# Two self attentions with scores issued first, and half of the output projection inside the second one

## The reference

```python
x = x + _L0_xattn_ref(_layernorm(x), ctx_1024, ...)
x = x + _L0_attn_ref(_layernorm(x), ...)     # "first attention": tokens of equal position attend to each other
x = x + _L0_ffn_ref(_layernorm(x), ...)      # 8 experts
x = x + _L1_xattn_ref(_layernorm(x), ctx_1024, ...)
x = x + _L1_attn_ref(_layernorm(x), ...)     # "second attention": the 64 tokens of a sample attend to each other
x = x + _L1_ffn_ref(_layernorm(x), ...)      # gated, inputs and weights rounded to FP4 by blocks of 16

def _L0_attn_ref(x, ...):
    ...
    scores = where(tril, q k^T / 4, -inf)
    out = softmax_one(scores) v              # e / (1 + sum e), no projection
def _L1_attn_ref(x, ...):
    ...
    out = softmax(q k^T / 4) v
    return out @ w_proj + b_proj
```

## Time and profile before

| what | us |
|---|---|
| median of 3 runs | 1421.54 (1418.49 to 1425.13) |
| the profiled execution | 1413.35 |
| its span in the trace | 1411.5 |
| PE busy | 1248.7 (88%) |
| DVE busy | 962.5 (68%) |
| ACT busy | 759.8 (54%) |
| POOL busy | 644.3 (46%) |

### The profile page before, as it was taken

One profiled execution on the slowest core, in us unless ns is written; L12 is line 12 of the kernel. 1 busy time (PEld: TensorE's weight loads), 2 busy tenths in 40 slices (PEclk: granted clock), 3 DMA queues, 4 the chain that ended last, 5 costly groups with the idle time before them and its releaser, 6 DMA issues. The chain is left out here.

```text
span 1411.5 us, 34690 instructions
## 1 busy us (share of the span) xinstructions
PE 1248.7 (88%) x12166; PEld 1044.0 (74%) x12166; DVE 962.5 (68%) x1990; ACT 759.8 (54%) x1379; POOL 644.3 (46%) x581
## 2 busy tenths in 40 slices
PE   5799999999999689449997799999999998667778
PEld 3588888888887557348885588888888887546446
DVE  5577777777777475465515677777777777576896
ACT  2577777777777211111224577777777776124121
POOL 2566656656654214042431556656656654315200
PEclk9999999999999885559999899999999999887999
DMA  6677777777765170435536677776776764100000
GB/s 199 173 205 196 176 194 188 181 195 182 185 170 126 42 55 2 127 119 177 187 131 190 176 201 182 186 201 176 182 205 176 183 173 111 35 1 3 0 4 26
DMA packets 106724, 198.31 MB, mean 140 GB/s; under 512 B 43662, under 2 KB 63791, under 8 KB 106641
## 3 DMA queue, kind: packets, MB, share of 16 engines
q1 hardware_dynamic: 105104, 193.32, 52.9%
q0 software_dynamic: 1536, 3.88, 0.9%
HBM read 88.26 MB, written 10.62 MB: 70 GB/s over the span
## 5 line engine op out<-in xcount | busy, mean ns | idle before, releaser
L844 POOL TENSOR_SCALAR cross_prob<-cross_prob,cross_inverse 128x1024 f32<-128x1024 f32 x256 | 288.8, 1128 | 344.4 <-DVE cross_inverse L593 344.4
L771 ACT ACTIVATE cross_prob<-cross_negated,cross_negmax 128x1024 f32<-128x1024 f32 x256 | 294.9, 1152 | 148.8 <-DVE cross_negmax L585 148.5
L585 DVE CUSTOM_DVE_ANT_0 cross_negated<-cross_scores,cross_bias 128x1024 f32<-128x1024 f32 x256 | 313.5, 1225 | 30.3 <-PE cross_scores L476 12.8
L489 PE MATMUL cross_turn<-ident,cross_prob 128*128 128x128 f32 x2048 | 269.6, 274 | 16.9 <-POOL cross_prob L844 12.9
L489 PEld LDWEIGHTS cross_turn<-ident,cross_prob 128*128 128x128 f32 x2048 | 239.7, 141 | 56.6 <-POOL cross_prob L844 16.7
L780 ACT COPY cross_probT<-cross_turn 128x512 f32<-128x512 f32 x256 | 149.6, 584 | 65.8 <-PE cross_turn L489 64.8
L476 PE MATMUL cross_scores<-cross_keys,cross_qbd 96*128 96x512 f32 x512 | 169.5, 413 | 12.6 <-POOL cross_qbd L836 12.6
L601 DVE COPY cross_probT<-cross_turn 128x512 f32<-128x512 f32 x256 | 175.6, 686 | 5.5 <-PE cross_turn L489 5.5
L824 POOL TENSOR_TENSOR cross_ctx_lo<-cross_raw,cross_ctx_hi 128x512 fp32r<-128x512 f32 x120 | 156.2, 1305 | 23.9 <-ACT cross_ctx_hi L747 23.8
L419 PE MATMUL cross_out<-cross_wv_hi,cross_ctx_lo 128*128 128x256 f32 x488 | 147.4, 302 | 0.0
L421 PE MATMUL cross_out<-cross_wv_hi,cross_ctx_hi 128*128 128x256 f32 x488 | 137.4, 282 | 0.0
(11 more groups left out here) (262 smaller groups left out, 2010.7 us busy)
## 6 DMA issues: line engine op xcount, KB each, us to landing
cross_keys<-cross_key_hi SPq DMA_DIRECT2D x512, 128.0 KB, 2.4
cross_raw<-in_ctxT SPq DMA_DIRECT2D x32, 1024.0 KB, 5.6
cross_keys<-cross_key_lo SPq DMA_DIRECT2D x256, 128.0 KB, 2.4
cross_bias<-bias_rows SPq DMA_DIRECT2D x32, 512.0 KB, 3.7
up_sb<-in_moe_w SPq DMA_DIRECT2D x8, 1024.0 KB, 6.1
down_sb<-in_moe_w SPq DMA_DIRECT2D x8, 1024.0 KB, 5.5
cross_stacked_q<-q_rows SPq DMA_DIRECT2D x90, 64.0 KB, 2.0
q_rows<-cross_negated SPq DMA_DIRECT2D x8, 256.0 KB, 2.4
```

What stands on the lines that cost most here:

```text
L489: last = pe.transpose(ps_t[part][:, k * P:(k + 1) * P], prob[n % 2][:, kt * P:(kt + 1) * P], ident)
L585: dve.tensor_tensor_reduce(negated[n % 2], ps_s[n % 2][:, :], bias_sb[par][:, :], -1.0, 3.0e38, ALU.add, ALU.min, negmax[:, n % 2:n % 2 + ...
L771: act.activation(prob[n % 2][:, :], negated[n % 2], ACT.Exp, bias=negmax[:, n % 2:n % 2 + 1], scale=-1.0, accum_out=total[:, n % 2:n % 2 + ...
L844: pool.tensor_scalar(prob[n % 2][:, :], prob[n % 2][:, :], inverse[:, n % 2:n % 2 + 1], 1.0, ALU.mult, ALU.mult).then_inc(prob_ready, 1)
```

## The change

In both attentions PE issues, in step i, scores(i+1) first, then turn(i-2), then weigh(i-3). In the second attention, where an `Ahead` object is passed in, four more things are done inside `self_block`: POOL adds the bias to x, one tile behind each divide, for all 8 tiles; the last division (tile 7) is DVE's; PE projects tiles 0 to 3 into the free score banks, two tiles behind weigh(4) and two behind weigh(5); DVE joins them and takes their statistics behind its last division, and POOL takes the two roots at its end. `gated_block` starts with normalize(0), and keeps project and join for tiles 4 to 7.

```diff
@@ self_block, PE
+            def project(i):
+                pe.wait_ge(shifted, NT)
+                for k in range(G):
+                    last = pe.matmul(score_banks[0][:, i, 0:D], oT[:, k, i * P:(i + 1) * P], ahead.w[:, k, :],
+                                     start=(k == 0), stop=(k == G - 1))
+                last.then_inc(projected, 1)
...
             def turn(i):
-                pe.wait_ge(prob_ready, i + 1)
+                if ahead is not None and i == NT - 1:
+                    pe.wait_ge(last_prob_ready, 1)
+                else:
+                    pe.wait_ge(prob_ready, i + 1)
...
             for i in range(NT + 3):
+                if i + 1 < NT:
+                    scores(i + 1)
                 if 2 <= i < NT + 2:
                     turn(i - 2)
-                if by_position and i + 1 < NT:
-                    scores(i + 1)
                 if i >= 3:
                     weigh(i - 3)
-                if not by_position and i + 1 < NT:
-                    scores(i + 1)
+                if ahead is not None and NT - 1 <= i < NT + 1:
+                    for tile in (2 * (i - NT + 1), 2 * (i - NT + 1) + 1):
+                        project(tile)
@@ self_block, DVE
+            def divide(i):
+                dve.wait_ge(inverse_ready, i + 1)
+                dve.tensor_tensor(prob[i % 3][:, :, :], prob[i % 3][:, :, :],
+                                  inverse[:, i % 2, :].unsqueeze(2).to_broadcast([P, M, queries]), ALU.mult
+                                  ).then_inc(last_prob_ready, 1)
+
+            def join(i):
+                dve.wait_ge(projected, i + 1)
+                dve.wait_ge(biased, i + 1)
+                dve.tensor_tensor(ahead.x[:, i, :], ahead.x[:, i, :], score_banks[0][:, i, 0:D], ALU.add).then_inc(joined, 1)
+                dve.wait_ge(joined, i + 1)
+                dve.bn_stats(ahead.stats[:, i, :], ahead.x[:, i, :]).then_inc(seen_by_norm, 1)
+                dve.wait_ge(seen_by_norm, 2 * i + 1)
+                dve.bn_aggr(ahead.moments[:, i, :], ahead.stats[:, i, :]).then_inc(seen_by_norm, 1)
...
+                if ahead is not None and i == NT:
+                    divide(NT - 1)
+                    for pair in range(2):
+                        join(2 * pair)
+                        join(2 * pair + 1)
+                        shift_variance(pair)
@@ self_block, POOL
+            def bias(i):
+                pool.tensor_tensor(ahead.x[:, i, :], ahead.x[:, i, :], ahead.b_row, ALU.add).then_inc(biased, 1)
+
+            def root(pair):
+                at = slice(2 * pair, 2 * pair + 2)
+                pool.wait_ge(stat_step, pair + 2)
+                pool.tensor_tensor(ahead.rstd[:, at], ahead.shifted[:, at], ahead.half_power[:, at], ALU.pow).then_inc(rooted, 1)
...
-                divide(i)
+                if ahead is None or i < NT - 1:
+                    divide(i)
+                if ahead is not None:
+                    bias(i)
+            if ahead is not None:
+                for pair in range(2):
+                    root(pair)
@@ gated_block, PE
-            for i in range(4):
-                project(i)
             turn_tokens(0)
@@ gated_block, DVE
-            dve.memset(power_[:, :], -0.5).then_inc(stat_step, 1)
-            for pair in range(2):
-                join(2 * pair)
-                join(2 * pair + 1)
-                shift(pair)
             normalize(0)
@@ gated_block, POOL
-            for i in range(4):
-                bias(i)
-            root(0)
-            root(1)
-            for i in range(4, NT):
-                bias(i)
             root(2)
             root(3)
```

More of the change, by code:

```diff
@@ L1021, in _, with self_block @@
                                   swapped[:, :, :, :].rearrange("p c h d -> p (c h d)"), ALU.add).then_inc(summed, 1)
[L1024 removed]
+def self_block(nc, tag, qkT, value, queries, causal, plus_one, quarter_mask, half_mask, ident, oT, ahead=None):
     with ExitStack() as ctx:
@@ L1157, in invert, with shift_variance @@
                 dve.reciprocal(inverse[:, a, :], total[:, a, :]).then_inc(inverse_ready, 1)
+            def divide(i):
[11 more added lines that the diff above has]
+                dve.bn_aggr(ahead.moments[:, i, :], ahead.stats[:, i, :]).then_inc(seen_by_norm, 1)
+            def shift_variance(pair):
+                at = slice(2 * pair, 2 * pair + 2)
+                dve.wait_ge(seen_by_norm, 4 * pair + 4)
+                dve.tensor_scalar(ahead.shifted[:, at], ahead.moments[:, at, 1], EPS, None, ALU.add).then_inc(stat_step, 1)
             def spread(i):
@@ L1687, in multiply, with __init__, gated_block @@
         return eng.tensor_tensor(self.by_block(out), self.by_block(self.v[:, at]), self.wide(self.scale, self.blocks_of(at)), ALU.mult)
-def gated_block(nc, tag, aT, w, b_row, x, moments, gate_upT, downT, ident, out):
+class Ahead:
+    def __init__(self, sb, w, b_row, x, moments):
+        self.w, self.b_row, self.x, self.moments = w, b_row, x, moments
+        self.stats, self.rstd, self.shifted, self.half_power = (sb(f"ahead_{n}", [P, NT] + more) for n, more in (
+            ("stats", [6]), ("rstd", []), ("shifted", []), ("half_power", [])))
+def gated_block(nc, tag, aT, ahead, gate_upT, downT, ident, out):
     with ExitStack() as ctx:
@@ L2051, in attend @@
                     loads.append((last[:, :, :], by_rows("self1_wp")))
+                ahead = Ahead(sb, last, rows[:, :], x, moments) if n == 1 else None
                 finish_last(loads)
@@ L2056, in attend @@
                 self_block(nc, f"self{n}_att", qkT, value, B if n == 0 else S, causal[:, :] if n == 0 else None, n == 0,
-                           quarter_mask, half_mask, eye, oT)
+                           quarter_mask, half_mask, eye, oT, ahead)
                 recycle_semaphores(nc)
                 if n == 1:
-                    gated_block(nc, "gated", oT, last, rows[:, :], x, moments, gate_upT, downT, eye, out)
+                    gated_block(nc, "gated", oT, ahead, gate_upT, downT, eye, out)
                 scope.pop()
```

35 lines of the change are left out of this document (20 added, 15 removed).

## The result

| | us |
|---|---|
| the changed kernel, median of 6 runs | 1409.74 (1407.22 to 1413.69) |
| the kernel before, median of 6 runs | 1419.41 (1413.44 to 1425.13) |
| ratio | 0.9935, 95% interval 0.9907 to 0.9963 |
| the changed kernel, profiled execution | 1413.69, span 1411.9 |

Two later comparisons of the same two kernels, 12 runs against 34 and 12 against 35, gave 0.9972 (0.9956 to 0.9988) and 0.9970 (0.9955 to 0.9984), 4.0 and 4.2 us of 1414.5 and 1414.8. All three intervals hold a change of 0.37 to 0.44%, 5.3 to 6.2 us; but that of the first alone, 5.3 to 13.2 us, does not hold the 4.0 and 4.2 us of the later two.

A forecast was written before the change was run, and what follows sets the result against it. It took PE, with POOL right behind, to bound the first attention, PE to wait in the second, and DVE to bound the gated block. 1.7 - 5.1 - 1.3 = -4.7 us from 1421.54 gave 1416.8, range 1411.5 to 1422.5.

The forecast's parts named there:

- First attention, +1.7: First attention: with scores ahead of turn, nothing covers the wait for POOL's queries; 1.7 us slower, bounds +1.0 to +2.5.
- Loop of the second attention, -0.9: Second attention's loop: scores first, but held by POOL's queries behind division and bias; shift(7) at 1292.78 instead of 1293.72.
- Tail: Second attention after scores(7): last turns, weighings and four projections; the attention ends at 1306.2, 0.5 us later than before.
- the clock should rise at the same place and hold: Second attention: PE's high clock assumed from scores(5) on, since the new order has shorter gaps; then -4.7 us stands.
- Block change and rounding: Gated block's start: block change stays 1.44 us; first rounding, no longer beside POOL's biases, gives -1.3 us.
- The sum, -4.7: Whole kernel: 1.7 for the first attention, -5.1 for tail and head together, -1.3 for the rounding; 4.7 us faster.
- its walk to the low end: Whole kernel: the forecast's best case, -7.3 us, with first attention +1.0 and the second attention's loop 2 us better.
- POOL does not hold the scores: Rival, both attentions: queries come early enough, first costs nothing, second runs DVE-bound; -8.3 us, 1413.2, chance 0.20.
- The clock stays low: Rival, second attention: low clock throughout, PE full at 4.9 us per tile; +6.3 us, 1427.8, chance 0.07.
- The joins and roots: Rival, gated block's head: joins or roots end last, or rounding no faster; gain only 0 to 3 us, chance 0.13.
- The rule on the clock: Second attention: if transposes do not count as PE busy, turns keep the clock low longer, moving -4.7 towards +6.3 us.

The follow-up runs named there:

- e6: The changed kernel with three query buffers instead of two, each spread one division earlier, in both attentions; ratio to the kernel before 0.9930.
- e4: The changed kernel with POOL's eight biases moved out of the second attention's loop; ratio to the kernel before 0.9938.
- e7: The changed kernel with biases out of the loop, three query buffers and unread products on PE together; 1401.97 us, ratio to the kernel before 0.9895.
- f3: The changed kernel with biases out of the loop and three query buffers, no added products; 1402.43 us, ratio to the kernel before 0.9896.
- e3: The full change again, unaltered, for a second trace; ratio to the kernel before 0.9972.
- f1: The changed kernel with two unread products on PE ahead of each of scores(5), (6) and (7) in the second attention; ratio to the kernel before 0.9949.
- n0: The kernel before, unchanged, timed against itself for a second trace; ratio 0.9999.
- n1: The kernel before, unchanged, timed against itself again for a third trace; ratio 1.0012.
- e1: The kernel before with scores ahead of turn in the first attention only; ratio to the kernel before 1.0009.
- e2: The changed kernel with the old order in the first attention; ratio to the kernel before 0.9968.
- e10: The full change once more, unaltered, for its size; ratio to the kernel before 0.9970.
- e5: The changed kernel with three unread products on PE ahead of each of scores(0) to (3) in the second attention; ratio to the kernel before 0.9956.

## Why the prediction was right and wrong

- **First attention, +1.7.** Right. Measured 1.6 in the stage (mean of seven traces with the new order and two buffers 54.2, of seven with the old 52.6). The starts of scores(5) to (7) were met within 0.1 us, and e6 shows the cause: with the queries earlier, the loss is gone. The first trace of before has 53.0, the longest of its order, so that the difference of the first two traces is only 1.2.
- **Loop of the second attention, -0.9.** The walk had shift(5) at 1283.79, shift(6) at 1288.44, shift(7) at 1292.78; the trace, less 4.41, has 1283.67, 1288.35 and 1293.49. The queue of POOL is what holds the scores, as said. The last step is 0.7 late: scores(7) ran at the low clock, 1.99 us instead of 1.12. So against the first trace of before the loop gave 0.2 us, 38.0 to 37.8, and not 0.9.
- **Tail.** The step of the walk that failed is "the clock should rise at the same place and hold". It rose 3 us later in the stage and fell again ahead of scores(7), in all four traces of this order with the biases in the loop. From sub(7) to normalize(0) I had 13.6 us (1307.64 - 1292.78 - 1.26); it was 15.3, 15.2, 14.2 and 15.3. Where the clock held, in e4, e6, e7 and f3, it was 13.5 each time; in e3, where it was back 3 to 4 us sooner than in the change, 14.2. Why it falls there is not shown. The two sizes, 0.7 and 1.7, make the 2.4 us by which normalize(0) is late: 53.1 instead of 50.7. This made the gain smaller than forecast, so it is not what put the time outside the range.
- **Block change and rounding.** 1.47 where 1.44 was said. From normalize(0) to the first product 13.5 became 12.2 us, -1.3 as walked, and from there to the end it is 85.2 to 85.3 in all traces but that of f1.
- **The sum, -4.7.** Its terms were met as +1.6, and -4.0 where -6.4 was said for all of the second half, against the trace that I had. But that trace was a short one. The four traces that hold the old second attention and gated block, before, n0, n1 and e1, have 154.5, 158.0, 154.6 and 157.7, mean 156.2; the four that hold the new, the change, e2, e3 and e10, have 150.5, 150.5, 149.5 and 150.5, mean 150.2. That is -6.0, and with +1.6 it makes -4.4 us, where e3 and e10 measured 4.0 and 4.2. By these traces two errors nearly cancelled, and that -4.7 lies so near to 4.0 and 4.2 is luck: 2.4 us for the clock that I took too high in the new kernel, and 1.7 (156.2 less 154.5) for a clock in my trace of the old one that two of its four traces do not have. The second is a mean of four and no more certain than that.
- **The time itself, and its range.** The step that put the result outside the range is "it lies 8 us below the median, so I apply the difference to the median: 1421.54 - 4.7". It took the median of three executions for the level and the stages of one trace for those of any. The kernel before had 1419.41 in the first comparison, and 1414.5 to 1417.0 in the later ones; its own touched stage alone differs by 3.5 us between traces. The first comparison shows 5 us more of a gain than the two later ones and than the stages. That excess stands in the number of the kernel before: the changed kernel had 1409.74, 1411.10 and 1409.11 in the three, the kernel before 1419.41, 1414.47 and 1414.83. From 1414.5 or 1414.8 the same -4.7 would have given 1409.8 or 1410.1. Why the kernel before was slower in the first comparison is open. Outside the touched stages the traces differ by more than the change is worth: the first attention starts between 518.9 and 525.2 us, and from its end to the second one it is 680.9 to 686.4. A range of -10 to +1 us was too narrow for such a level (and its walk to the low end adds to -7.4 and not -7.3); the chances, 0.65 for within 0.5%, were those of the walk and not of a sample of six.
- **The rivals.** "POOL does not hold the scores" did not come, but e6 makes it true: forecast -8.3, measured 9.9 less. "The clock stays low" came in part, 1.7 + 0.7 us; in full it is seen only in f1's trace, 9 us longer, but three pairs of added products of 2.0 us each stand in that. (Its shift(7) at 1294.5 would be 1294.2 by three of its 4.9 us from 1279.45.) The joins and roots did not come last: the last root ended 1.35 us ahead of the last copy.
- **The rule on the clock.** The Trainium skill, TensorE: Matmul & The Clock Gate, Part 4: PE-mode transpose, says that a transpose does not count as PE being busy in the same way. In e6 the clock stayed at 1.0 for over 20 us in which a third of PE's work was turns; in f1 it stayed at 0.5 for steps in which the other matmuls filled 5.1 of 7.47 us. Neither bears the rule out as what decides here; no run isolates the turns.

## What to carry to other kernels

When a piece of work is moved from ahead of a product to behind it, ask whose lateness it had covered: here the turn had hidden POOL's queries in the first attention, and in the second the wait moved from the turn to the same queue. Give the producer one more buffer before reordering the consumer; in e6 this alone took the queries' wait away in both places. And take two or three traces of the kernel before: if its clock has two courses, one trace holds the price of a change no better than the difference between them, 3.5 us here. Check the level in the same way: here a median of three executions lay 7 us above that of 34 in a later comparison.

## What the runs showed of the hardware that I had not expected

- One program has the granted clock in two courses in the same stage: up at 21 us in two executions of before, not before 38 us in a third; 3.5 us between them.
- The clock stayed at 0.50 while PE was shown busy: in n0 for 22 us with 19.98 of them busy (windows from 14 to 36 us of the stage), in f1 for 24 us with 22.5 busy (24 to 48), among them 7.0 us without a gap (from 1286.02). In e5 and e7 three products per step, placed at the start of the stage, stood ahead of a rise at 8 us. What the clock turns on is not settled.
- DVE's division of tile 7 took 1.76 us where it started 0.05 us behind the start of a bias on POOL (the change), and 1.22 where it started 0.08 ahead of it (e3). POOL's two biases beside it took 2.40 and 2.42 us, where two in e4, ahead of that division, took 1.42. Which engine starts first decides which one is held up:

```profile
1303.79 1.76 DVE L1176 TENSOR_TENSOR self_att_prob<-self_att_prob,self_att_inverse 128x1024 f32<-128x1024 f32 x1
1303.74 2.40 POOL L1291 TENSOR_TENSOR x<-x,self_row 128x256 f32<-128x256 f32 x2
```

```profile
1303.31 1.22 DVE L1176 TENSOR_TENSOR self_att_prob<-self_att_prob,self_att_inverse 128x1024 f32<-128x1024 f32 x1
1303.39 2.42 POOL L1291 TENSOR_TENSOR x<-x,self_row 128x256 f32<-128x256 f32 x2
```
